# Global attention with a windowed two-layer network on one core: x rows loaded first, weights late, splits and residual on GpSimd, a new merge order

## The reference

```
h = layernorm(x) * (1 + ca) + sa                 # per batch, from silu(c) @ wmod
q, k, v = h @ W + b, each reshaped (b, 16 heads, 8, 512)
attn = softmax((k^T v) * temperature)            # 512 x 512 per head, heads of 8 dims
x = x + ga * (q @ attn)                          # global attention, "a"
h = layernorm(x) * (1 + cb) + sb
for 2 layers:                                    # windowed attention and FFN, "b"
    h' = shift_token(h);  q, k, v = h' @ wqkv    # 8 heads of 64
    q, k = rotary(l2norm(q)), rotary(l2norm(k))
    h = h + softmax over a window of 64 and the one before (q k^T) v @ wo
    h' = layernorm(shift_token(h)) * g + b
    h = h + (a * gelu(g)) @ w2,  a, g = h' @ w1
x = x + gb * h
```

## Time and profile before

| | |
|---|---|
| median of three executions | 1298.11 us |
| profiled execution, its time | 1305.42 us |
| its span, first to last instruction | 1303.6 us |
| busy PE / DVE / ACT / POOL | 1065.7 / 976.1 / 923.0 / 466.8 us |
| mean granted TensorE clock | 0.895 of full speed |

### The profile page before, as it was taken

The page is one execution under the profiler, slowest core; times in us unless marked ns, Lnnn a source line. Parts: engine busy times, 40 slices in busy tenths (PEclk is TensorE's granted clock), DMA queues, the critical chain, the costliest instruction groups (busy, mean ns, idle before and its releaser), DMA issues. The chain is left out here.

```text
span 1303.6 us, 23771 instructions
## 1 busy us (share of the span) xinstructions
PE 1065.7 (82%) x8124; PEld 530.6 (41%) x8124; DVE 976.1 (75%) x1985; ACT 923.0 (71%) x2782; POOL 466.8 (36%) x537
## 2 busy tenths in 40 slices
PE   4078878988878789878888889898888988888987
PEld 3021334334323433343234356455446455534463
DVE  3096988897788789787996875876795688677755
ACT  1087689879777987797888587486568566766684
POOL 3000332052004312320142573455285266354660
PEclk8575889988888999698788999989999989999999
DMA  4612031211310402113001011011011011010110
GB/s 153 193 62 75 1 117 43 72 52 36 99 40 16 128 17 94 40 36 102 27 7 24 0 30 29 1 37 30 9 29 30 2 37 30 9 29 1 30 30 17
DMA packets 24647, 59.15 MB, mean 45 GB/s; under 512 B 2832, under 2 KB 3024, under 8 KB 23376
## 3 DMA queue, kind: packets, MB, share of 16 engines
q1 hardware_dynamic: 23394, 55.53, 14.4%
q10 hardware_dynamic: 1134, 2.10, 0.5%
HBM read 23.98 MB, written 18.87 MB: 33 GB/s over the span
## 5 line engine op out<-in xcount | busy, mean ns | idle before, releaser
L843 ACT ACTIVATE E<-psum,neg_max 128x512 f32<-128x512 f32 x512 | 348.3, 714 | 100.0 <-DVE neg_max L1137 77.5
L1137 DVE TENSOR_REDUCE neg_max<-psum 128x2 f32<-128x1024 f32 x256 | 306.9, 1213 | 86.4 <-PE psum L429 85.3
L776 POOL TENSOR_TENSOR work<-work,rot_work 128x512 f32<-128x512 f32 x128 | 162.7, 1272 | 183.5 <-DVE rot_work L1206 182.8
L429 PE MATMUL psum<-v_rows,k_rows 32*128 32x512 f32 x512 | 137.2, 556 | 99.6 <-ACT E L843 45.8
L484 PE MATMUL psum<-wqkv_sb,hs 128*128 128x512 f32 x384 | 195.7, 636 | 11.5 <-DVE rot_work L1206 3.8
L939 ACT ACTIVATE rot_work<-psum,neg 128x128 f32<-128x128 f32 x512 | 184.3, 407 | 26.4 <-DVE neg L1228 18.5
L789 POOL TENSOR_TENSOR rot_work<-rot_work,rz 128x512 f32<-128x512 f32 x128 | 133.2, 1042 | 186.4 <-DVE rz L1233 186.4
L762 POOL TENSOR_TENSOR qz<-qT,rz 128x32 f32<-128x32 f32 x128 | 31.2, 245 | 397.4 <-DVE rz L1141 393.6
L438 PE MATMUL psum<-E,qz 128*32 128x512 f32 x1024 | 164.2, 718 | 0.0
L429 PEld LDWEIGHTS psum<-v_rows,k_rows 32*128 32x128 f32 x512 | 54.7, 205 | 253.5 <-issue 127.3
L784 POOL TENSOR_TENSOR work<-work,rn 128x512 f32<-128x512 f32 x128 | 134.2, 1062 | 29.4 <-DVE rn L1091 29.3
(11 more groups left out here) (121 smaller groups left out, 1671.6 us busy)
## 6 DMA issues: line engine op xcount, KB each, us to landing
work<-v_al SPq DMA_DIRECT2D x16, 512.0 KB, 4.4
work<-v_al SPq DMA_DIRECT2D x16, 384.0 KB, 6.2
k_scr<-hi SPq DMA_DIRECT2D x16, 256.0 KB, 2.9
k_scr<-lo SPq DMA_DIRECT2D x16, 256.0 KB, 3.4
v_scr<-hi SPq DMA_DIRECT2D x14, 256.0 KB, 3.1
v_scr<-lo SPq DMA_DIRECT2D x14, 256.0 KB, 3.4
k_rows<-k_scr SPq DMA_DIRECT2D x16, 192.0 KB
v_rows<-v_scr SPq DMA_DIRECT2D x14, 192.0 KB
```

Source lines behind the costliest of these rows:

```text
L429: pe.matmul(bank, k_rows[r:r + 32, hh, P * j:P * (j + 1)], v_rows[r:r + 32, b % 2, hh, :], start=True, stop=True).then_inc(full, 1)
L776: pool.tensor_tensor(qk[s][:, i, w, :], qk[s][:, i, w, :], sinp[s][:, n % 2, :], ALU.add).then_inc(rot_sum[s], 1)
L843: act.activation(E[:, (b * NG + g) % E_RING, 2 * half + m, :], pair[:, m], ACT.Exp, bias=neg_max[:, n, m:m + 1], accum_out=z[:, n, m:m + 1 ...
L1137: dve.tensor_reduce(neg_max[:, n, :], pair, AX.X, ALU.max, negate=True).then_inc(max_ready, 1)
```

## The change

- SP loads x of batches 1 to 7 before it waits for `k_parts` of batch 0. The weights are loaded only when all of `v_rows` of batch 0 has landed.
- The cast to `hi`, the subtraction for `lo` and the addition of the residual to `x_sb` are issued on POOL instead of DVE. DVE keeps the read of PSUM into `kf` and the multiplication by the gate. New semaphores `kf_ready` and `hi_ready` link the two engines. In POOL's stream a split follows the scaling steps 5 and 7 of a batch, and the residual follows step 0 of the next one.
- POOL does the two splits of batch 0 before it scales the rotary tables.
- The four gate broadcasts are steps of the a stream, after score steps 16, 18, 20 and 22 of batch 0.
- The arrival of `v_rows` has one semaphore for each quarter, as that of `k_rows` has; a quarter of score steps waits for its own pieces.
- `ORDER` and `BANKS` are new. Up to its last a letter, PE's string has 218 x letters before and 180 after; DVE's 204 and 169, ACT's 207 and 174, POOL's 116 and 96. A batch of x or y has 94 letters in PE's string.

The core of the diff (of the tables one line; the added `a_split` and `a_residual` are those of POOL):

```
 ORDER = {
     "PE": (
-        "aaaaaaaaaaaaaaaaaaaaaaaaaaaaaaaaaaaaaaaaaaaaaaaaaaaaaaaaaaxaxxxxxxxxxaaaaxxaaaaxaaaaxxxaaaaaxxxaaaaa"
+        "aaaaaaaaaaaaaaaaaaaaaaaaaaaaaaaaaaaaaaaaaaaaaaaaaaaaaaaaaaaaaaaaaaaaaaaaaaaaaaaaxaaaaaaaaaaaxaaaxxaa"
...
+        def rows_landed(eng, s, b, hh):
+            passed(eng, s[hh], 16 * len(PIECES[hh]) * (b + 1))
...
 def a_scores(b, n):
-                if n == 0:
-                    passed(pe, v_in, (b + 1) * 16 * V_LOADS)
                 if n % (STEPS // HQ) == 0:
-                    passed(pe, k_in[hh], (b + 1) * 16 * K_LOADS[hh])
+                    rows_landed(pe, v_in, b, hh)
+                    rows_landed(pe, k_in, b, hh)
...
+                        if b == 0 and n in GATES_AT:
+                            a_gates(*divmod(GATES_AT.index(n), 2))
...
             for l in range(L):
                 load(rot[:, l], rotary, s_rot)
+            for b in range(1, B):
+                a_load(b, x_loaded)
             a_parts(0, 0)
             for hh in range(HQ):
                 a_keys_in(0, hh)
-            for b in range(1, B):
-                a_load(b, x_loaded)
+            for hh in range(HQ):
+                rows_landed(sp, v_in, 0, hh)
             load(wqkv_sb[:], wqkv)
...
+            def a_split(b, n):
+                pool.wait_ge(kf_ready, 2 * b + n + 1)
+                passed(pool, (k_out, v_out)[n], b * 16 * 4)
+                pool.tensor_copy(hi[:, n], kf[:]).then_inc(hi_ready, 1)
+                pool.wait_ge(hi_ready, 2 * b + n + 1)
+                pool.tensor_tensor(lo[:, n], kf[:], hi[:, n].bitcast(F32), ALU.subtract).then_inc((k_parts, v_parts)[n], 1)
+
+            def a_residual(b):
+                passed(pool, o_read, b + 1)
+                pool.tensor_tensor(x_sb[:, b], x_sb[:, b], o_gated[:], ALU.add).then_inc(x2_ready, 1)
...
                     for g in range(NG):
+                        if b and g == 1:
+                            a_residual(b - 1)
+                            yield
                         a_weigh(b, g)
                         yield
+                        if b + 1 < B and g in (5, 7):
+                            a_split(b + 1, (g - 5) // 2)
+                            yield
...
-                    split_link(dve.tensor_tensor(kf[:], src, bv_bc.unsqueeze(1).broadcast_to([P, J, D]), ALU.add))
-                dve.tensor_copy(hi[:, n], kf[:]).then_inc(free, 1)
+                    ins = dve.tensor_tensor(kf[:], src, bv_bc.unsqueeze(1).broadcast_to([P, J, D]), ALU.add)
+                ins.then_inc(free, 1)
                 done(dve, ("a", b, "kv"[n]))
-                dve.tensor_tensor(lo[:, n], kf[:], hi[:, n].bitcast(F32), ALU.subtract).then_inc((k_parts, v_parts)[n], 1)
-                if n:
-                    split_end()
+                dve.sem_inc(kf_ready, 1)
...
-                passed(dve, o_read, b + 1)
-                dve.tensor_tensor(x_sb[:, b], x_sb[:, b], o_gated[:], ALU.add).then_inc(x2_ready, 1)
```

More of the change, by code:

```diff
@@ L46 @@
 SPLIT_AT = {"k": 13, "v": 17}
-K_LOADS = [1, 2, 2, 2]
-V_LOADS = sum(K_LOADS)
+GATES_AT = [16, 18, 20, 22]
+PIECES = [[(q, n, (q + hh) % HQ) for q, n in ((0, HQ - hh), (HQ - hh, hh)) if n] for hh in range(HQ)]
 STREAMS = 2
@@ L92 @@
+        "xxxyyyyyyyyxxyyxyyyxyyyyyxyxyxxyxxyyxyyxxxxyyyxxxxyyxxyyyyyyyyyyyxyxxxxxxxyxyyyyyyxyyyyyyyyxyyyyxxyx"
+        "yxyyyxxyxxxyyyyy"
     ),
     "ACT": (
[L94 to L97, removed]
@@ L388, in modulation, with a_gates @@
                 last.then_inc(full, 1)
-            def gate_rows():
+            def a_gates(g, n):
                 pe.wait_ge(s_gcol, 1)
-                for g in range(2):
-                    for n in range(2):
-                        bank, full = take(pe, ("gate", g, n))
-                        for i in range(4):
-                            c = g * B + 4 * n + i
-                            last = pe.matmul(bank[:, D * i:D * (i + 1)], gate_col[:, 0, c:c + 1].broadcast_to([D, P]),
-                                             ident[:], start=True, stop=True)
-                        last.then_inc(full, 1)
+                bank, full = take(pe, ("gate", g, n))
+                for i in range(4):
+                    c = g * B + 4 * n + i
+                    last = pe.matmul(bank[:, D * i:D * (i + 1)], gate_col[:, 0, c:c + 1].broadcast_to([D, P]),
+                                     ident[:], start=True, stop=True)
+                last.then_inc(full, 1)
             def a_transpose(b):
@@ L627, in _ @@
             a_project(0, "v")
-            gate_rows()
             a_scores(0, 0)
@@ L809, in b_stream @@
                             yield
+            a_split(0, 0)
+            a_split(0, 1)
+            pool.wait_ge(s_first, 16 * 2)
+            pool.wait_ge(s_rot, 16 * L)
+            for l in range(L):
+                for w in range(2):
+                    sc = scale_bc[:, l, w, :]
+                    pool.tensor_tensor(rot[:, l, :, w, 0, :], rot[:, l, :, w, 0, :],
+                                       sc.unsqueeze(1).broadcast_to([P, J, DH]), ALU.mult).then_inc(s_tables, 1)
+                    for a in range(2):
+                        r = rot[:, l, :, w, 1, 32 * a:32 * a + 32]
+                        pool.tensor_tensor(r, r, sc[:, 32 - 32 * a:64 - 32 * a].unsqueeze(1).broadcast_to([P, J, 32]),
+                                           ALU.mult).then_inc(s_tables, 1)
             merge([a_stream(), b_stream(0), b_stream(1)], ORDER["POOL"])
@@ L1009, in _ @@
             values_first()
-            gates()
             values_first_in()
```

159 lines of the change are left out of this document (71 added, 88 removed).

## The result

The changed kernel takes 1283.8 us (median of four, 1281.05 to 1290.5) beside 1298.87 for the kernel before: ratio 0.9894, 95% interval [0.9866, 0.9922]. It is faster by about 1.1%, somewhat more than half of the 1.84% that was forecast. The profiled execution took 1282.93 us with a span of 1280.9.

A forecast was written before the change was run, and what follows sets the result against it. PE, DVE and ACT were taken to share the bound, none alone. Span: 117.9 until x enters + 524 mixed + 637.7 network = 1279.6 us against 1303.6; median 1274, range 1248 to 1295.

The forecast's parts named there:

- the start: Before the first exponential: it comes at 41.8 us, after ACT's issuing of v rows, 23 us earlier than 64.78.
- Attention alone: Global attention before x enters: 41 steps at 1.85 us, 75.9 us, plus gates 2.4; x enters at 117.9 us.
- The mixed stretch: Attention together with x, 215 steps and 3.83 layers: 524 us, with ends at 509 and 540.
- Half the relief: Mixed stretch: half of the 19.9 us of work taken off DVE is gained, 524 us instead of 534.
- my two splits of the price: Mixed stretch: a step at 1.85 and a layer at 37.0 us give 539.5; 1.53 and 52.4 give 528.6.
- The ring of waits: Mixed stretch: PE waits for ACT 36.6 us, ACT for DVE 36.3, DVE for PE 29.9; all three share the bound.
- The cost of POOL beside DVE: Mixed stretch: POOL's moved work slows DVE through shared access; 3 us taken of a possible 19, inside the half relief.
- The network alone: Windowed network, x with y, after the mixed stretch: 12.17 layers at 52.4 us, 637.7 us, 42 more than before.
- Rival 4: Relief void and 0.81 layers at full price, start as forecast: span 1296 us, median 1291, about no change; chance 12%.
- Rival 1: Better fill by the new order: mixed stretch 508 us, network 621, span 1247, median 1242; chance 20%.
- Rival 2: Start gains less, first exponential at say 52 us or x loads late: 10 us more, median 1284; chance 15%.
- Rival 3: POOL's splits hold up the scaling steps in the mixed stretch: span 1332 us, median 1326, slower; chance 8%.

The follow-up runs named there:

- the start alone: Kernel before with only x loaded first, weights late and a wait for each quarter of v rows: 0.9804, 1273.62 us.
- POOL alone: Kernel before with only cast, subtraction and residual addition moved to POOL; old loads, order and wait for all of v: 1.0014.
- the new order alone: Kernel before with only the new merge order and gates as steps of the a stream; splits, residual and loads as before: 1.0099.
- the changed kernel in the old order: Changed kernel with ORDER and BANKS of before and the gates ahead of the merge again: 0.981, 1276.27 us.

## Why the prediction was right, and where not

- **Direction and mechanism of the start: right.** 23 us forecast for the first exponential, 24.6 in the trace, 25 by the start alone. But the reason for 41.8 was half right. ACT's issuing ends at 40.03 (27.06 + 12.97) and the first exponential follows at once, at 40.13; the score itself waited for v rows until 37.14, ten microseconds after their issue. Without ACT's issuing it could have come under 1 us earlier. The cast took 0.61 us (0.63 taken) and the subtraction 1.26.
- **A term was missing.** The x loads were counted only as traffic. That the layernorm of batch 1 stands two steps into DVE's queue and would wait for x was not seen; with the x loads left behind, the whole gain is lost and more (1.0066). The sum was not hurt, as the change moves them.
- **Attention alone:** x was to enter at 117.9 and did at 111.7; 41 steps took 74.6 us, 1.82 each. The entry came earlier as the first score (37.1) was earlier than 62.6 - 23 = 39.6, and gates and part of the step cost did not show.
- **The mixed stretch: the size of one term was off.** 524 us forecast, 529.5 measured. "Half the relief" fails: 10 us were put at it, and it is nothing that can be measured, by two pairs of kernels (1.0014 for POOL alone, and 0.9906 against 0.9894). The other of my two splits of the price, a layer at 52.4 and a step at 1.53 with nothing gained, gives 528.6. The old and the new order bear it out: from 576.9 to 536.5 us for 0.81 layers, 50 a layer. By this x is hardly cheaper beside the attention than beside y. The ring of waits was to turn too, with PE for ACT in the place of ACT for DVE. It did not: in the mixed stretch PE's scores wait 33.5 us for ACT (36.6 before) and ACT 27.8 for DVE (36.3), but DVE 41.5 for PE (29.9).
- **The cost of POOL beside DVE.** The 3 us taken for it can't be seen: DVE's maxima take 1214 ns in the mean, 1213 before, with 39 us more of POOL's work.
- **A wait that the sum does not have.** The forecast put nothing on k rows coming late behind the first batch. In the changed kernel PE waits for them twice in the mixed stretch, 9.8 us together, at the first scores of batches 3 and 5:

```profile
243.82 0.79 PE L436 MATMUL psum<-v_rows,k_rows 32*128 32x512 f32 x2 [7.01 <-DMA k_rows<-k_scr]
400.91 0.79 PE L436 MATMUL psum<-v_rows,k_rows 32*128 32x512 f32 x2 [2.84 <-DMA k_rows<-k_scr]
```

  With the new order alone it is 5.5 us; in the kernel before, the start alone and the changed kernel in the old order PE has no such wait in this stretch. So a part of what the new order costs may lie here and not in the price of a layer. The 50 us a layer include these waits, and no run takes them apart.
- **The network alone: right.** 637.7 forecast, 639.7 measured, 52.6 us a layer.
- **What the order costs.** The sum had the network 42 longer, the later entry 9 and the gates 2, against a mixed stretch 54 shorter of which 10 were relief: a loss of some 9 us, 0.7%. It measures 1.0% alone and 0.8% in the changed kernel. In 0.81 layers, 40 us were saved in the middle (576.9 to 536.5) and 48 paid at the end (591.6 to 639.7). That the order costs this much is measured; which part of it are layers and which the waits for k rows is not.
- **Rivals.** Rival 4 had the relief void, which is true, but took the dear split of the price with it. Rivals 1, 2 and 3 are out: the last stretch is 639.7, the first score came at 37.1, and PE waited for POOL's `qz` 5.2 us in all where it had waited 1.3.
- **The span came out by luck in part.** It was forecast at 1279.6 and is 1280.9, since the entry of x was 6.2 us too late in the sum, the mixed stretch 5.5 too short and the network 2.0 too short.
- **The conversion to a median.** The median was forecast at 1274 and is 1283.8. The last step, that the profiled execution stands 0.56% over the median, held for the kernel before and not for the changed one: 1282.93 profiled, 1283.8 median. Both kernels spread by 0.4 to 0.7% between executions, so such an offset of one execution should not have been carried over; the ratio forecast, 0.982, lies outside the measured interval for the most part for that reason. With the two spans alone the ratio is 0.9826 too; the profiled executions flatter the change by half a percent.

## What to carry to other kernels

A microsecond taken from a busy engine is worth what stands behind it in the other queues: here 29 us added at DVE's maxima cost 25, of which 16 to 19 came from the places themselves and the rest with a lower granted clock, and 26 us of casts, subtractions and residual additions removed beside them gave none. Whoever adds work to an engine to see who paces the kernel should compare the granted clock of both kernels before reading the difference. Before a load is brought forward, look what else in the first few instructions of each queue waits for the loads it overtakes; the wait next in line can take the gain back. And a new merge order should be timed apart from the edits that it comes with: this one cost 1%, half as much as the edits beside it gained.

## What was not expected of the hardware

Two score matmuls on different 32-row blocks overlap: 512 of them make 133.8 us of busy time at a mean of 557 ns each. Issued again on the same rows and bank, one costs more: 88 of them, with a median of 494 ns, added 29.4 us of busy time between the first score and the last residual, 0.33 us each where one of the 512 costs 0.26. Row transfers out of DRAM into 32 to 128 partitions were slow beside the wide ones: seven v transfers of 1 MB in all were issued from 28.12 us in the kernel that waits for all of them, and the last had landed only when its first score ran at 55.45, with 1 MB of k rows beside them, 2 MB in some 30 us; the first of the weights, 1.5 MB in one transfer, landed 6.5 us after its issue in the changed kernel.
